# Causal attention stage: the sums' products moved in front of a run of the next half's value products

## The chip, the cores and the metric

The kernel runs on one core of a Trainium2 chip. The time is microseconds on the device from the start to the end of one execution; a lower one is better. Beside it stands one profiled execution, whose rows are read here.

## The reference, cut to what matters

`x` is 4 sequences of 1024 tokens with 512 channels. A layer with causal self-attention (16 heads of 32 channels), cross-attention to 64 context rows and a feed-forward block is followed by a second layer with a gate. Only the first attention is touched by the change:

```python
xn1 = _ln(x, g1, be1)
q, k, v = xn1 @ Wq + bq, xn1 @ Wk + bk, xn1 @ Wv + bv        # per head
scores = jnp.where(causal_mask, q @ k.T / scale, -jnp.inf)
attn = jax.nn.softmax(scores, axis=-1)
x = x + (attn @ v) @ W1 + b1
```

Everything is float32.

## The kernel before

**Tiling.** The causal stage handles 16 groups `g` (4 sequences by 4 groups of four heads). A group has two halves `c2` of 512 query tokens. For a half, key blocks `j` of 128 keys (4 of them in half 0, 8 in half 1) and heads `i` (4) give a scores product `sc` (line 805, transposed: keys on the partitions), then `ex` on ScalarE (line 918) writes the exponentials. Blocks on the diagonal are masked first by VectorE (`low`, line 1034), and their products are narrower: 512, 384, 256 and 128 columns.

**Values.** `pv` (line 817) is a run of four products, one per head: 128 keys by 32 channels, each written to its own 32 partitions of PSUM bank 7. TensorE so works in groups of 32 columns there, while all its other products of this stage use 96 to 128. The profile has two records for each such product, so a `pv` is x8.

**Sums.** The exponentials of block 0 are written into `esum[c2][i]` (`es` in the profile), those of the other blocks into a ring of 8 tiles `er`. GpSimd adds each ring tile onto `es` (line 677). When a half is complete, `fin` (line 826, index `f = 2 * g + c2`) multiplies a matrix of ones with the four `es` tiles, again four products of 128 by 32 into four groups of 32 partitions, 512 columns each. Then comes a chain: ScalarE copies the result into `esum[c2][0]` (line 929), `f0` (SyncE's queue) moves four rows of it into a small tile (line 609), `f1` is the reciprocal on VectorE (line 1043), `f1d` and `f2` spread it through DRAM into the tile `rs` (lines 613 and 619), `f3` on GpSimd multiplies the attention output by it (line 683), `f3d` stores 256 KB (line 624). The exponentials of block 0 of the same half of the next group overwrite `es`, so the first of them waits for the landing of `f0` (semaphore `d_cmp`, lines 916 and 917).

**Other work of the stage.** Row maxima of the coming group: products `mx` (line 762), reduced by VectorE (lines 1023 and 1027), turned by `mxT` (line 775). Projections `pj` and values `vm` in three passes (lines 55 to 57), normalised tokens transposed (`lnT`, line 739), and `stack`, DMAs of 256 KB, three per call, that rearrange queries and keys (line 599).

**Order.** All five engines walk one list, `order1()`, sorted by a planned time whose unit is one group; each takes its own steps from it, in order. `attn_steps` gives the steps of a half with weights and `spread` lays them evenly between the half's start and end (half 0 of group `g` is planned from `g` to `g + CUT`, half 1 from there to `g + 1`). `fin` and its chain are placed by fixed distances after the end of their half. `banks1` walks the same list and gives each PSUM use of the stage one of seven banks, the one free longest; a use waits for the release of the one before it in its bank (`free1`).

Of the kernel before, what the change touches and what calls it, by code (L numbers as in the profile page):

```python
# [72 lines left out]
def spread(start, end, steps):  # L73

    steps = list(steps)
    total, done, out = sum(c for _, c in steps), 0.0, []
    for s, c in steps:
        out.append((start + (end - start) * done / total, s))
        done += c
    return out  # L80


def ln_times(b, qt, ld, lnT):

    d = lnT - ld
    out = [(ld, ("ld", b, qt))] + [(ld + (0.36 + 0.06 * i) * d, ("st", b, qt, i)) for i in range(2)]
    out += [(ld + 0.5 * d, ("va", b, qt)), (ld + 0.56 * d, ("rs", b, qt))]
    out += [(ld + (0.68 + 0.08 * i) * d, ("nm", b, qt, i)) for i in range(2)]
    for kp in range(2):
        at = lnT + 0.05 * kp  # L90
        out += [(at, ("lnT", b, qt, kp)), (at + 0.01, ("lnh", b, qt, kp)), (at + 0.03, ("lnl", b, qt, kp))]
    return out


def proj_times(g, c2, wq, start, end):
    out = [(start + (end - start) * k / 4, ("pj", g, c2, wq, k)) for k in range(KT)]
    return out + [(end, ("pjh", g, c2, wq)), (end + 0.02, ("pjl", g, c2, wq))]


def max_steps(g, c2):  # L100
    for r, (ti, h0, per, c0, w, diag) in enumerate(MAXU):
        if ti // 4 == c2:
            yield ("mx", g, r), per * w + 100
    if c2:
        yield ("mxm", g), 300


def attn_steps(g, c2):

    nj = 4 * c2 + 4  # L110
    for j in range(nj + 1):
        for i in range(4):
            if j < nj:
                yield ("sc", g, c2, j, i), 512 - max(0, 128 * (j - 4 * c2)) + 60
            else:
                yield ("none",), 240
            if i == (3 if j > 4 * c2 else 2) and j:
                yield ("pv", g, c2, j - 1), 800 * (512 - max(0, 128 * (j - 1 - 4 * c2))) / 512
    yield ("none",), 200

# [3 lines left out]
CUT = (0.292, 0.27, 0.283, 0.294)  # L124
# [12 lines left out]
def order1():  # L137

    at0 = lambda us: (us - 72) / 58
    t = [(at0(a), s) for a, s in ((1.5, ("zld", 0)), (1.6, ("wld", 0)), (1.7, ("wld", 1)), (1.8, ("zld", 1)), (24.5, ("wld", 2)),  # L140
                                  (18, ("wh", 0)), (22, ("wh", 1)), (32, ("wh", 2)), (31, ("zp",)), (70, ("oh1",)), (15, ("msk",)), (20, ("ohc",)))]
    for qt in range(4):
        at, T0 = 4 + 2.5 * qt, 8 + 2.6 * qt
        t += [(at0(a), s) for a, s in ((1 + 0.1 * qt, ("ld", 0, qt)), (at, ("st", 0, qt, 0)), (at + 0.1, ("st", 0, qt, 1)),
                                       (at + 1, ("va", 0, qt)), (at + 1.2, ("rs", 0, qt)), (at + 2.6, ("nm", 0, qt, 0)),
                                       (at + 2.7, ("nm", 0, qt, 1)))]
        for kp in range(2):
            t += [(at0(T0 + 1.3 * kp), ("lnT", 0, qt, kp)), (at0(T0 + 1.3 * kp + 0.6), ("lnh", 0, qt, kp)),
                  (at0(T0 + 1.3 * kp + 1.2), ("lnl", 0, qt, kp))]
    for j in range(3):  # L150
        t += [(at0((18.5, 25, 45)[j] + (1.6, 1.6, 3.1)[j] * m), ("wb", j, m)) for m in range(4)]
    for u in range(13):
        at = 15.5 + 3.5 * u if u < 4 else 32 + 3 * (u - 4) if u < 8 else 45 + 3 * (u - 8)
        t += [(at0(at), ("z", u)), (at0(at + 2.5), ("ze", u))]
        if u < 4 or u in (8, 12):
            t.append((at0(at + 4), ("zo", u)))
    for b in range(1, NB):
        for qt in range(4):
            t += ln_times(b, qt, 4 * b + LN_LOAD[qt], 4 * b + LN_TURN[qt])
    for g in range(16):  # L160
        r = g % 4
        cut = CUT[r]
        at = [at0(a) for a in PROJ_0] if g == 0 else [g + a for a in (PROJ_1 if g == 1 else PROJ[r])]
        for c2 in range(2):
            for wq in range(2):
                n = 2 * c2 + wq
                t += proj_times(g, c2, wq, at[n], at[n] + (0.05 if g < 2 else PROJ_LONG[r]))
                back = g - 2 + (CUT[(g - 2) % 4] if n == 0 else CUT[(g - 2) % 4] + (1 - CUT[(g - 2) % 4]) * 0.54 if n == 1 else 1) + 0.03
                t.append((at[n] + 0.1 if g == 0 else max(at[n] + PROJ_LONG[r] + 0.07, back), ("stack", g, c2, wq)))
        if g % 2 == 0:  # L170
            for sp in range(4):
                s, d = (at0(VALUES_0[sp]), 0.05) if g == 0 else (g + VALUES[r // 2][sp], VALUES_LONG)
                t += spread(s, s + d, [(("vm", g // 2, sp, i), 1) for i in range(4)])
                t.append((s + d, ("ve", g // 2, sp)))
        m0, m1, end = (at0(46), at0(54), MAX_0) if g == 0 else [g + a for a in (MAX_1 if g == 1 else MAX[r])]
        t += spread(m0, m1, max_steps(g, 0)) + spread(m1, end, max_steps(g, 1))
        for c2, a in enumerate((m1, end)):
            t += [(a + 0.04, ("mxT", g, c2)), (a + 0.06, ("tq", g, c2)), (a + 0.09, ("tqd", g, c2))]
        for c2 in range(2):
            end = g + (1 if c2 else cut)  # L180
            steps = spread(g + cut * c2, end, attn_steps(g, c2))
            t += steps
            for a, s in steps:
                if s[0] == "sc" and s[3] >= 4 * c2 :
                    t += [(a + 0.014, ("low", *s[1:])), (a + 0.028, ("ex", *s[1:]))]
                elif s[0] == "sc":
                    t.append((a + 0.001, ("ex", *s[1:])))
            t += [(end + 0.02, ("sao", g, c2)), (end + 0.08, ("fin", 2 * g + c2))]
            t += [(end + a, (s, 2 * g + c2)) for a, s in ((0.14, "f0"), (0.26, "f1"), (0.3, "f1d"), (0.42, "f2"), (0.62, "f3"), (0.69, "f3d"))]
    t += order2()  # L190
    t.sort(key=lambda p: p[0])
    return t
# [152 lines left out]
def program(nc, A, out):  # L345
    top = ExitStack()
    with top:
# [84 lines left out]
        bt = cols[:, col_at["bt"]:col_at["bt"] + 4]  # L432
        BO = 7
        O1 = order1()
        Q.bank, Q.before, Q.last = banks1(O1)
        O1 = [s for _, s in O1]
# [1743 lines left out]
```

## Time and profile before

| | us |
|---|---|
| median of 3 runs | 2281.62 (2280.57 to 2282.13) |
| profiled execution | 2281.93 |
| its span | 2280.1 |
| causal stage, first value product to the last adds and sums | 114.4 to 984.7 |

The page's first part gives busy time by engine; its second part cuts the span into 40 slices, one digit of busy tenths each; its fourth part follows the chain of work that ended last. In the timeline each row is a start, a length, an engine, a line, an operation, what it writes and reads, and how many records were merged; brackets hold idle time of the engine before it and what ended it. Matmul records overlap, so the distance between starts, and not the length, is what a product occupies.

### The profile page before, as it was taken

How to read it: one execution, taken by the hardware profiler on the slowest of the kernel's cores; microseconds unless marked ns; L12 is line 12 of the kernel's file. 1: busy time of each engine (PE TensorE's matmuls, PEld its weight loads, DVE VectorE, ACT ScalarE, POOL GpSimd, SP SyncE). 2: the span in 40 equal slices, each digit the busy share in tenths (PEclk: the TensorE clock that was granted, in tenths of full speed). 3: DMA queues.
4: the chain of work that ended last, by engine and by line, in shares of the span. 5: the costliest groups of instructions: out<-in, count | busy, mean ns of one | idle time of the engine just before them, and what ended most of it. 6: DMA issues, size and time to landing. Idle time of an engine off the chain costs nothing.

```text
span 2280.1 us, 32164 instructions
## 1 busy us (share of the span) xinstructions
PE 2158.8 (95%) x11590; PEld 1604.1 (70%) x11590; DVE 1407.5 (62%) x3349; ACT 861.8 (38%) x1598; POOL 933.1 (41%) x943
## 2 busy tenths in 40 slices
PE   7999999999999997889999998999999999999996
PEld 5666666666656664467777776888887887888784
DVE  5577776876786678456666677443455546454546
ACT  4155655655565554533443333221211121121113
POOL 1067777777777777653333332001021201111212
PEclk9999999999999998899999999999999999999998
DMA  7655545555564564211111221320111121111101
GB/s 233 78 82 95 95 78 89 104 90 81 94 113 76 84 94 123 71 52 59 58 56 60 79 94 42 120 79 28 61 60 65 70 74 61 65 61 65 42 28 51
DMA packets 106323, 177.34 MB, mean 78 GB/s; under 512 B 18334, under 2 KB 23454, under 8 KB 106160
## 3 DMA queue, kind: packets, MB, share of 16 engines
q1 hardware_dynamic: 106164, 175.29, 33.1%
q8 instruction: 91, 1.49, 0.3%
q14 instruction: 68, 0.56, 0.1%
HBM read 83.67 MB, written 40.13 MB: 54 GB/s over the span
## 4 chain that ended last, share of the span: by engine, by line
PE 82%; DVE 7%; ACT 4%; issue 3%; POOL 2%; DMA 1%; SPq 0%; POOLq 0%; ACTq 0%; DVEq 0%
PE psum L55 19%; PE psum L56 18%; PE psum L57 18%; PE psum L817 6%; PE psum L762 6%; PE psum L805 5%; PE psum L720 1%; DVE psum L1023 1%; PE psum L826 1%; ACT sx L1369 1%; PE psum L1323 1%; PE psum L739 1%; PE psum L1315 1%; PE psum L1264 1%; ACT pT L1396 1%
## 5 line engine op out<-in xcount | busy, mean ns | idle before, releaser
L677 POOL TENSOR_TENSOR es<-es,er 128x512 f32<-128x512 f32 (+3 forms) x640 | 588.7, 955 | 266.5 <-PE psum L817 241.5
L918 ACT ACTIVATE er<-psum 128x512 f32<-128x512 f32 (+3 forms) x640 | 278.5, 471 | 299.8 <-DVE psum L1034 192.3
L1023 DVE CUSTOM_DVE_ANT_0 psum<-psum,mask_ts 128x384 f32<-128x384 f32 (+3 forms) x512 | 249.2, 502 | 151.7 <-PE psum L762 149.5
L805 PE MATMUL psum<-qs,ks 100*128 100x512 f32 (+3 forms) x768 | 251.0, 364 | 22.3 <-DVE mx L1023 18.7
L762 PE MATMUL psum<-ks,qs 96*128 96x512 f32 (+3 forms) x768 | 259.1, 369 | 5.8 <-DVE mx L1023 3.1
L1873 ACT ACTIVATE fy<-psum,cols 128x512 f32<-128x512 f32 x128 | 88.2, 689 | 452.4 <-PE psum L57 451.9
L762 PEld LDWEIGHTS psum<-ks,qs 96*128 96x128 f32 x768 | 139.6, 190 | 111.6 <-issue 32.9
L1027 DVE TENSOR_REDUCE mx<-psum 128x1 fp32r<-128x512 f32 x256 | 175.5, 685 | 59.5 <-PE psum L762 58.6
L55 PE MATMUL psum<-fh,hh 128*128 128x512 f32 x512 | 201.0, 393 | 7.1 <-DVE hl L1974 7.1
L55 PE MATMUL psum<-fah,fh 128*128 128x512 f32 x512 | 203.0, 397 | 0.0
L1972 DVE CAST hh<-fy 128x512 fp32r<-128x512 f32 x128 | 60.9, 476 | 229.8 <-ACT fy L1873 229.4
L57 PE MATMUL psum<-fah,fl 128*128 128x512 f32 x512 | 200.1, 391 | 0.0
L56 PE MATMUL psum<-fal,fh 128*128 128x512 f32 x512 | 199.9, 390 | 0.0
L57 PE MATMUL psum<-fh,hl 128*128 128x512 f32 x512 | 199.4, 390 | 0.0
L56 PE MATMUL psum<-fl,hh 128*128 128x512 f32 x512 | 199.3, 389 | 0.0
L805 PEld LDWEIGHTS psum<-qs,ks 100*128 100x128 f32 x768 | 143.0, 193 | 69.0 <-DVE mx L1023 31.3
L1238 POOL TENSOR_TENSOR pp<-pp,small 128x1024 f32<-128x1024 f32 x32 | 61.1, 1911 | 266.2 <-DVE small L1504 266.2
L1769 POOL TENSOR_TENSOR et<-et,vpb 128x512 f32<-128x512 f32 x24 | 35.4, 1477 | 284.9 <-ACT et L1899 284.9
L1034 DVE TENSOR_TENSOR psum<-psum,mask_st 128x128 f32<-128x128 f32 x512 | 138.2, 303 | 21.8 <-PE psum L805 21.1
L817 PE MATMUL psum<-er,v 128*32 128x512 f32 (+3 forms) x1280 | 137.8, 486 | 0.6 <-ACT er L918 0.4
L55 PEld LDWEIGHTS psum<-fh,hh 128*128 128x128 f32 x512 | 96.1, 188 | 28.9 <-DVE hl L1974 9.5
L57 PEld LDWEIGHTS psum<-fah,fl 128*128 128x128 f32 x512 | 96.4, 188 | 20.6
(258 smaller groups left out, 4593.0 us busy)
## 6 DMA issues: line engine op xcount, KB each, us to landing
qs<-stage SPq DMA_DIRECT2D x96, 256.0 KB, 5.7
ks<-stage SPq DMA_DIRECT2D x96, 256.0 KB, 8.2
rs<-rs_d SPq DMA_DIRECT2D x32, 256.0 KB
sa_d<-rs SPq DMA_DIRECT2D x32, 256.0 KB, 2.1
sx<-sa_d SPq DMA_DIRECT2D x8, 1024.0 KB, 5.7
xt<-in_x SPq DMA_DIRECT2D x32, 256.0 KB, 6.0
x_d<-xt SPq DMA_DIRECT2D x32, 256.0 KB, 2.0
fw<-in_Wf SPq DMA_DIRECT2D x16, 512.0 KB, 5.2
```

The source lines that it names most:

```text
L55: e.matmul(dst, lh, rh, start=start, stop=False)
L56: e.matmul(dst, lh, rl, start=False, stop=False)
L57: return e.matmul(dst, ll, rh, start=False, stop=stop)
L677: e.tensor_tensor(es, es, er, ALU.add).then_inc(s_add.sem, 1)
L762: t = e.matmul(bank1(*s)[:, v * wd:v * wd + wd], Q.qs[par][0:96, i, 128 * ti:128 * ti + 128], Q.ks[par][0:96, i, c0:c0 + wd], start=True, ...
L805: t = e.matmul(ps[:, off:512], Q.ks[par][0:100, i, 128 * j:128 * j + 128], Q.qs[par][0:100, i, 512 * c2 + off:512 * c2 + 512], start=True, ...
L817: e.matmul(bank[BO][32 * i:32 * i + 32, off:512], values(g)[:, j, h:h + 32], src[:, off:512], start=j == 0, stop=j == nj - 1).then_inc(s_p ...
L918: e.activation(dst, bank1("sc", g, c2, j, i)[:, off:512], ACT.Exp, scale=SCALE).then_inc(s_freeS.sem, 1)
L1023: t = e.tensor_tensor_reduce(out=ps, in0=ps, in1=mask_ts[:, 512 - wd:512], scale=1.0, scalar=-3e38, op0=ALU.add, op1=ALU.max, accum_out=mx ...
L1027: e.tensor_reduce(mx[:, at:at + 1], bank1(*s)[:, 0:wd], AX, ALU.max).then_inc(s_red.sem, 1)
L1034: e.tensor_tensor(ps, ps, mask_st[:], ALU.add).then_inc(s_low.sem, 1)
L1873: e.activation(y[:], ring3(("h", c, m)), ACT.Relu, bias=col("bf1", m), scale=1.0).then_inc(s_r3.sem, 1)
```

## The change

`fin` leaves its fixed place (0.08 group after the end of its half). It is now yielded by `attn_steps` of the next half, with weight 0, directly ahead of one of that half's `pv` runs: ahead of block 1 in half 0, and of block 2 in half 1. Its chain keeps its distances from `fin` (0.06, 0.18, 0.22, 0.34, 0.54 and 0.61 group). The last `fin` (31) and its chain stay where they were. The order of all other steps among themselves stays the same on every engine; since `banks1` walks the changed list, most uses get another bank (1332 of 1664).

```diff
+FIN_BESIDE = (1, 2)
+FIN_AFTER = (0.06, 0.18, 0.22, 0.34, 0.54, 0.61)
 def attn_steps(g, c2):
     nj = 4 * c2 + 4
...
             if i == (3 if j > 4 * c2 else 2) and j:
+                if j - 1 == FIN_BESIDE[c2] and (g or c2):
+                    yield ("fin", 2 * g + c2 - 1), 0
                 yield ("pv", g, c2, j - 1), 800 * (512 - max(0, 128 * (j - 1 - 4 * c2))) / 512
...
+    attn_order = {(g, c2): spread(g + CUT[g % 4] * c2, g + (1 if c2 else CUT[g % 4]), attn_steps(g, c2))
+                  for g in range(16) for c2 in range(2)}
...
-            steps = spread(g + cut * c2, end, attn_steps(g, c2))
+            steps = attn_order[g, c2]
...
-            t += [(end + 0.02, ("sao", g, c2)), (end + 0.08, ("fin", 2 * g + c2))]
-            t += [(end + a, (s, 2 * g + c2)) for a, s in ((0.14, "f0"), (0.26, "f1"), (0.3, "f1d"), (0.42, "f2"), (0.62, "f3"), (0.69, "f3d"))]
+            t.append((end + 0.02, ("sao", g, c2)))
+            if g == 15 and c2:
+                t.append((end + 0.08, ("fin", 31)))
+            fin = end + 0.08 if g == 15 and c2 else next(a for a, s in attn_order[g + c2, 1 - c2] if s[0] == "fin")
+            t += [(fin + a, (s, 2 * g + c2)) for a, s in zip(FIN_AFTER, ("f0", "f1", "f1d", "f2", "f3", "f3d"))]
```

## Rows read from the trace of the kernel before

**Rows 1.** The page: busy time, and two lines of its 40 slices.

```profile
PE 2158.8 (95%) x11590; PEld 1604.1 (70%) x11590; DVE 1407.5 (62%) x3349; ACT 861.8 (38%) x1598; POOL 933.1 (41%) x943
...
PE   7999999999999997889999998999999999999996
...
PEclk9999999999999998899999999999999999999998
```

**Rows 2.** The page: the chain that ended last, by engine.

```profile
PE 82%; DVE 7%; ACT 4%; issue 3%; POOL 2%; DMA 1%; SPq 0%; POOLq 0%; ACTq 0%; DVEq 0%
```

**Rows 3.** Busy time in stretches of the causal stage (records in brackets).

```profile
376.00:588.00 212.00, 207.74 (x1289) 136.76 (x1289) 155.30 (x516) 122.32 (x258) 160.95 (x179) 1.00 0.56 92
588.00:800.00 212.00, 207.48 (x1286) 136.44 (x1285) 155.33 (x513) 121.81 (x257) 160.57 (x179) 1.00 0.55 92
800.00:930.00 130.00, 113.56 (x638) 69.32 (x637) 94.24 (x268) 68.42 (x151) 96.56 (x100) 0.89 0.47 94
930.00:985.00 55.00, 48.03 (x198) 23.79 (x196) 24.71 (x51) 23.84 (x49) 37.52 (x35) 0.91 0.22 77
```

**Rows 4.** Timeline of TensorE around one sums run, of the half before.

```profile
590.52 0.40 PE L56 MATMUL psum<-xl,wqh 128*128 128x512 f32 x1
590.76 0.39 PE L57 MATMUL psum<-xh,wql 128*128 128x512 f32 x1
590.99 0.34 PE L805 MATMUL psum<-qs,ks 100*128 100x384 f32 x1
591.25 1.07 PE L826 MATMUL psum<-es,sm 128*32 128x512 f32 x8
592.25 0.44 PE L762 MATMUL psum<-ks,qs 96*128 96x384 f32 x1
592.53 0.52 PE L805 MATMUL psum<-qs,ks 100*128 100x384 f32 x2
```

**Rows 5.** Timeline of TensorE: an ordinary 384-column pitch, and value runs of 512 and 128 columns.

```profile
589.93 0.34 PE L762 MATMUL psum<-ks,qs 96*128 96x384 f32 x1
590.11 0.34 PE L805 MATMUL psum<-qs,ks 100*128 100x384 f32 x1
...
561.13 1.06 PE L817 MATMUL psum<-er,v 128*32 128x512 f32 x8
562.12 0.50 PE L762 MATMUL psum<-ks,qs 96*128 96x512 f32 x1
...
534.54 0.43 PE L817 MATMUL psum<-er,v 128*32 128x128 f32 x8
534.90 0.66 PE L762 MATMUL psum<-ks,qs 96*128 96x128 f32 x4
```

**Rows 6.** The line of the sums' products: ns min/median/max.

```profile
L826 PE MATMUL psum<-es,sm x256: 592/617/1062, 124.9 to 984.7; 128*32 128x512 f32 x128
```

**Rows 7.** Timeline of TensorE, 641.2 to 652 us: all rows with idle time.

```profile
643.34 0.44 PE L805 MATMUL psum<-qs,ks 100*128 100x384 f32 x1 [0.28 <-ACT es L918]
...
644.53 0.45 PE L805 MATMUL psum<-qs,ks 100*128 100x384 f32 x1 [0.76 <-DVE mx L1023]
...
648.16 0.63 PE L739 MATMUL psum<-ident,xr 128*128 128x128 f32 x4 [0.29 <-ACT xr L857]
...
650.98 0.50 PE L762 MATMUL psum<-ks,qs 96*128 96x512 f32 x1 [0.45 <-DVE mx L1023]
```

**Rows 8.** Timelines of SyncE's queue, TensorE and ScalarE around `f0` of half 11.

```profile
429.71 2.25 SPq L599 DMA_DIRECT2D ks<-stage  x3
...
432.77 0.57 SPq L609 DMA_DIRECT2D small<-es  x1
...
437.51 0.53 PE L817 MATMUL psum<-er,v 128*32 128x384 f32 x4
...
443.05 0.60 ACT L918 ACTIVATE es<-psum 128x512 f32<-128x512 f32 x1 [1.16 <-PE psum L805]
```

**Rows 9.** Half 27: issue of its `f0`, and the one exponential that waited for it.

```profile
854.37 0.58 SPq L609 DMA_DIRECT2D small<-es  x1
...
863.50 1.09 ACT L918 ACTIVATE es<-psum 128x512 f32<-128x512 f32 x2 [2.20 <-DMA small<-es]
```

**Rows 10.** The page: DMA issues by kind, the last number from issue to landing.

```profile
ks<-stage SPq DMA_DIRECT2D x96, 256.0 KB, 8.2
...
sa_d<-rs SPq DMA_DIRECT2D x32, 256.0 KB, 2.1
```

**Rows 11.** Timeline of GpSimd, 372 to 392 us.

```profile
372.19 1.26 POOL L683 TENSOR_TENSOR rs<-sao,rs 128x512 f32<-128x512 f32 x1
373.42 4.47 POOL L677 TENSOR_TENSOR es<-es,er 128x256 f32<-128x256 f32 x8
384.19 7.93 POOL L677 TENSOR_TENSOR es<-es,er 128x384 f32<-128x384 f32 x11 [6.30 <-PE psum L817]
```

**Rows 12.** Who waited for whom in the causal stage.

```profile
ACT es L929 <- PE psum L826: 9.7, 18, 1.2
...
ACT er L918 <- POOL es L677: 5.1, 10, 1.1
```

## The prediction

> **What bounds the kernel now.** I read the page first, for the engine that carries the span: TensorE is busy 95% of it, at full clock in nearly every slice [rows 1], and it makes 82% of the chain that ended last [rows 2]. An average says little about the stage that is changed, so the second view is busy time by stretch. Between 376 and 800 us TensorE is busy 207.74 of 212 us and 207.48 of 212 us, 98%, at a granted clock of 1.00 (the 2.4 GHz level), while VectorE has 73%, ScalarE 58% and GpSimd 76% [rows 3]. There a nanosecond that TensorE no longer needs is mostly a nanosecond of time. From 800 to 985 us it is busy 113.56 of 130 and 48.03 of 55 us, 87%, with the clock at 0.89 to 0.91 [rows 3]: other engines and transfers set the pace in part, and a saving is worth less.
>
> Third, the timeline of TensorE, for what one sums run costs. In it, only distances between starts count. The run of half 17 starts at 591.25 and the next product at 592.25 [rows 4].
>
> **The edit on TensorE.** The same 32 `fin` runs of 8 records are issued, so no product is removed. What goes is that a run of 32-column products stands alone between products of the full width. I price both situations.
>
> Alone: the product ahead of the run starts at 590.99 and is 384 columns wide; two such products otherwise stand 0.18 us apart (589.93 to 590.11, [rows 5]), but the run starts 0.26 us later: 0.08 on entering. The run holds the engine for 1.00 us (591.25 to 592.25). The product behind it, again 384 wide, is followed after 0.28 us (592.25 to 592.53) instead of 0.18: 0.10 on leaving [rows 4, 5]. Together 1.18 us.
>
> In a longer run: the trace has no sums run joined to a value run, so I bound it. Each record lasts 0.617 us and the eight together 1.07 [rows 4, 6], so the last starts about 0.45 us after the first: four products' first passes take 0.45, and eight records in a stream 0.90. That gives 1.18 - 0.90 = 0.28 us saved per join. Another way: a value run of 128 columns occupies 0.36 us (534.54 to 534.90), one of 512 columns 0.99 (561.13 to 562.12) [rows 5]; that is 0.63 us for 384 columns, 1.64 ns each, so 512 columns stream in 0.84 and 0.15 us is fixed. Then 1.18 - 0.84 = 0.34 us per join. From below: if what is fixed belongs to each group of four products whatever stands beside it, the 0.15 stays, and if entering and leaving are only late weight loads that a joined run has as well, nothing is saved: 0. Nothing in the rows makes a join dearer than standing apart, since both runs then have the same shape. I take 0.29, nearest to the value that comes from the starts inside a run.
>
> The Trainium skill has another account of the end of such a run ("TensorE: Matmul & The Clock Gate", section "The cost: per-tile semaphore tail"): increments serialise, about 25 + 4.7 per tile + 26.3 ns per increment. By that page a value run with its four increments would have a tail of 149 ns and a sums run with its single one 70 ns, an estimate from the page's formula. The trace doesn't bear that difference out: both occupy the same 0.99 to 1.00 us [rows 4, 5].
>
> Joins: all but the last of 32, so 31. Those of halves 0 to 27 land in the saturated part: 28 x 0.29 = 8.1 us. Halves 28 to 30 are in the last stretches at 87%: between 0 and 3 x 0.34 = 1.0; I take 0.3. Sum: -8.4 us.
>
> **What gives some back.** First, filler. Each `fin` moves later by 6 to 18 us: half 17's from 591.25 to its join, and half 11's to 437.51, where `pv` of block 1 starts [rows 8]. Between the two places TensorE arrives 1.18 us earlier at products whose banks VectorE or ScalarE must free. Where it already idles there, the idleness grows. In one group out of four it does: 0.28, 0.76, 0.29 and 0.45 us of idle time between 643 and 651 us, mostly for VectorE [rows 7]. The whole 1.18 us could turn into idle time there, of which the join then pays back nothing; in the other groups the idle rows are few, since all idle time of 424 us is 8.8 us [rows 3]. The loss is between 0 and 4 x 1.18 = 4.7 us; VectorE is busy only 73%, so it catches up in part, and I take 1.0.
>
> Second, the chain behind `fin`. Everything in it moves with it: the ScalarE copy, `f0`, `f1`, `f1d`, `f2`, `f3` and `f3d`. On VectorE the reciprocal keeps its 0.12 group behind `f0`; on ScalarE the copy waits for its products as it did 18 times for 9.7 us in all [rows 12], on an engine with 42% to spare. On GpSimd, `f3` of every first half leaves the densest part of the second half (372.19, with adds right behind it) and falls into the 6.30 us that GpSimd idles before the next group's first add [rows 11]: 1.26 us of relief per group for an engine that ScalarE waited for by 5.1 us in all [rows 12]. I count no gain for that. `f3` of a second half moves one block later in the same kind of row, price nothing.
>
> Third, the wait on `f0`. For a second half, its landing must come before the first exponential of the next group's second half. With half 11: `fin` now starts at 437.51 minus its own length, thus on the old clock about 437.5, the four products and the copy take 1.7 us (1.07 + 0.6), `f0` is issued near 439.3, and the exponential stands at 443.05 [rows 8]: 3.8 us are left. Unloaded, 2.1 us are enough even for 256 KB; but the small transfer goes behind `stack` transfers that take 8.2 us to land [rows 10]. In half 27 it took from 854.37 to about 863.5, 9.1 us, and the exponential waited 2.20 [rows 9]. Key transfers issued at 429.71 [rows 8] plus 8 to 10 us land near 439 to 441, so an `f0` issued at 439.3 lands hardly later than one issued at 432.77 did, except for one new thing: `f3d` of the first half, 256 KB, now goes into SyncE's queue between `stack` and this `f0`. Three stack transfers of 256 KB are issued in 2.25 us and take 8.2, so one such transfer in the backlog is worth 0.7 to 2.7 us. Added waiting per group is then between 0 and about 2 us of ScalarE, 0 to 30 us over 15 groups at the far end; what reaches TensorE is smaller, since the value products of block 0 come several products later. By the slack of 3.8 us I expect it to show only where stack's backlog was deepest, as in half 27: 0.4 us in sum.
>
> Fourth, banks. The new assignment is as crowded as the old: the same seven banks, the same steps. A `fin`'s own bank is now wanted soon after it, by scores products of block 3 about 1.3 to 2 us behind the old start of `pv` block 1; the added 0.9 us of the joined run keeps that just clear of the 1.7 us until the copy is done. Between -1 and +1.5 us; I take 0.
>
> **Sum.** -8.4 + 1.0 + 0.4 = -7.0 us. The profiled execution (2281.93; span 2280.1, 1.8 around it) would become 2274.9, and it stands 0.3 above the median of the runs, 2281.62, which becomes 2274.6.
>
> **The rivals.** Changes of up to 0.2%, 4.6 us, can hardly be told from none.
>
> *A: half of it given back.* The join saves 0.28, but TensorE waits for VectorE in more groups than the one in four. 1.18 us of lost filler in half of the 28 places, of which a quarter sticks, is 4 us: -8.4 + 4 to 6, so 2277 to 2279. For it speaks that VectorE is the next in the chain [rows 2] and the four idle rows [rows 7]; against it, that idle time is 2% [rows 3].
>
> *B: the change doesn't do what it says.* Fixed time belongs to each group of four products, or new weights in a joined run come late; a join saves 0 to 0.07 us, 31 x 0.07 = 2.2, less the 1.4 given back: 2280 to 2282. Against it: inside a run the second passes follow at 0.45 us though they have their own weights [rows 4, 6]. The Trainium skill's semaphore tail is of this kind: only a sums run's own 70 ns would be recovered.
>
> *C: slower, by the wait on `f0`.* One mechanism: `es` is free later than the first exponential of block 0. With `f3d` ahead and 9 us as in half 27 [rows 9] it would land at 448 instead of 443. It decides once the added wait exceeds 8.4 / 15 = 0.56 us of TensorE per group; at 1 us it gives 2281.6 - 8.4 + 1 + 15 = 2289. For it: one wait is there already [rows 9]. Against it: transfers ahead were issued 8 us earlier and drain in the meantime.
>
> **How the numbers follow.** Forecast 0.70, with its own range 2271.5 (31 x 0.34 = 10.5 and nothing given back gives 2271.1) to 2277; A 0.14; B 0.07; C 0.09, of which 0.02 stays within the bound. The range: 2271.5 to 2279.5 takes in the forecast and A and leaves out B, C and the edge. Faster by over 0.2% (below 2277.06): the forecast and some of A, 0.75. Within: most of A, B and the rest of C, 0.18. Slower: 0.07.
>
> **What the changed profile would show.** Right: in TensorE's timeline 31 places where x8 of line 826 is followed by x8 of line 817 with no full-width product between, the two starting about 0.9 us apart, and one entering and one leaving for both; the stage ending 7 to 8 us earlier, and all later stages as long as before. A: more idle rows ended by line 1023 between a half's start and the join. B: the value run starts 1.0 us or more behind the sums run. C: `ACT es L918` waiting for `DMA small<-es` in many groups instead of one. The forecast is wrong if the join shows a third pass that comes later than 0.45 us, or if ScalarE's copies now hold a bank that scores products of block 3 need.

## The result, and the profile after

Before: 2278.78 us, the median of 20 runs (2270.25 to 2285.31). After: 2283.54 us, the median of 20 (2278.21 to 2288.64). The ratio is 1.0025, 95% interval 1.0016 to 1.0033: the change costs 5.7 us of 2279, where 7.0 us of gain were forecast. (Here and below a ratio is taken over all runs, and the us beside it are that ratio on the median before. The difference of two medians can be another by up to 2 us; here it is 4.8. The twenty runs before have a median 2.8 us under that of the three runs the forecast started from, which doesn't change its sign.) The profiled execution after took 2283.22 us with a span of 2281.4 and a mean granted clock of 0.979; before it was 2281.93, 2280.1 and 0.984.

All line numbers after are 11 higher. The page after: busy time and chain by engine, to be read against [rows 1, 2], and two kinds of transfer against [rows 10].

```profile
PE 2162.4 (95%) x11590; PEld 1613.8 (71%) x11590; DVE 1402.9 (61%) x3349; ACT 861.8 (38%) x1598; POOL 934.2 (41%) x943
...
PE 83%; DVE 7%; ACT 4%; issue 3%; POOL 2%; DMA 1%; POOLq 0%; SPq 0%; DVEq 0%; ACTq 0%
...
ks<-stage SPq DMA_DIRECT2D x96, 256.0 KB, 7.1
...
sa_d<-rs SPq DMA_DIRECT2D x32, 256.0 KB, 6.5
```

The same 11590 products keep TensorE busy 3.6 us longer: work didn't go, it got slower. (The stores of the normalised halves land in 6.5 us instead of 2.1, since they now go among `stack`'s transfers. No compute engine waits for them; SyncE's own queue does, 12 times for 19.2 us in all, before 6 times for 12.0.)

The join itself does what it was said to. TensorE's timeline of half 17 after, which answers to [rows 4]:

```profile
592.72 0.28 PE L816 MATMUL psum<-qs,ks 100*128 100x256 f32 x1
592.93 1.06 PE L837 MATMUL psum<-es,sm 128*32 128x512 f32 x8
593.82 0.83 PE L828 MATMUL psum<-er,v 128*32 128x384 f32 x8
594.58 0.33 PE L816 MATMUL psum<-qs,ks 100*128 100x128 f32 x1
```

The value run starts 0.89 us behind the sums run, with 0.90 forecast, and no product of another shape stands between; the trace has 31 such joins. So look for where the gain went. Busy time in the stretches of [rows 3], with the granted clock as the third number from the end:

```profile
376.00:588.00 212.00, 207.81 (x1286) 138.60 (x1285) 154.62 (x510) 122.36 (x259) 160.06 (x176) 0.99 0.56 92
588.00:800.00 212.00, 207.81 (x1285) 138.68 (x1284) 154.60 (x512) 122.27 (x258) 160.09 (x176) 0.99 0.56 92
800.00:930.00 130.00, 116.77 (x626) 71.72 (x627) 90.06 (x256) 66.82 (x149) 97.07 (x99) 0.84 0.43 92
930.00:985.00 55.00, 47.57 (x193) 23.33 (x191) 23.37 (x50) 23.09 (x47) 37.26 (x34) 0.91 0.21 73
```

In each of the two full stretches the clock is 0.99 instead of 1.00 and TensorE gets through a few products fewer; from 800 to 930 us it is 0.84 instead of 0.89, and TensorE is busy 3.2 us longer with 12 records fewer.

Both kernels issue the same other products in the same order, so they can be lined up. The table is worked out from the traces: when a product starts, against the same product of the profiled execution before (us; the columns are the time there). Each kernel was profiled twice more for it.

```
                    427    849    870    984   2200   total of the run
before, again 1     0.0    0.0   +1.5    0.0   -0.3   2281.66
before, again 2    -0.9   +1.6   +1.6   -7.6   -5.4   2277.93
after              -3.0   -2.9   +0.3   +0.4   -0.2   2283.22
after, again 1     -1.6   -2.3   +1.8   -2.3   -2.3   2279.64
after, again 2     -2.0   -2.7   +1.1   +2.3   +2.5   2284.78
first halves only  -4.6   -6.7   -7.4  -16.9  -15.0   2268.35
```

Three things are to be seen. The kernel after is ahead by 2 to 3 us by 427 us and hardly more at 849, though 16 joins lie between. Between 849 and 870, the first half of group 14 and the start of its second, it loses 3.2 to 4.1 us (the kernel before 0.0, 1.5 and 0.0). And one execution of the kernel before gets 9 us in one place behind 870 that the others don't, so a single profile can't tell 5 us here; the verdicts below come from many runs.

Cut at the first scores product of each half, the same line-up says what a join does where. Differences in the length of halves against the profiled execution before, in us, summed over the groups named; the last four rows are kernels of the experiments below:

```
                    first halves of groups       second halves  1st half of  2nd half of
                    odd 3 to 13   4,8,12   6,10  3 to 13        group 2      group 14
before, again 1         0.0        0.0    +0.1     0.0            +0.1          +0.5
before, again 2         0.0        0.0    +2.6    +0.1            -1.4          -8.8
after                  -0.7       +0.9    +3.0    -3.4            -0.9          +0.3
after, again 1         -0.7       +1.0    +2.2    -3.4            -0.5          -1.7
after, again 2         -0.7       +1.0    +2.2    -3.6            -0.7          +1.5
first halves only       0.0        0.0    +0.8    -3.3            -3.5         -10.8
old banks              -0.2       +1.1    +5.3     0.0            -0.3          +2.3
before, late split      0.0        0.0    +0.4    +0.6            -3.5         -10.9
filler back            -0.7       +0.9    +1.4    -3.5            -0.6          +1.9
```

Eleven joins in second halves give 3.4 to 3.6 us, 0.31 each (unevenly: 1.0 in groups 6 and 10, 0 to 0.3 in the others). Eleven joins in first halves cost 2.4 to 3.2 us: those of odd groups give 0.12 each, those of groups 4, 8 and 12 cost 0.3 each, and those of groups 6 and 10 cost 2.2 to 3.0 together. What the last two columns show comes and goes without the change: the first half of group 2 is 3.5 us shorter in the kernel "before, late split", whose order is that of the kernel before up to group 14.

Where the rest of the 0.29 goes is to be seen in group 9 (and in 5, but not in 3, 7 and 11). TensorE after, then before:

```profile
595.84 0.60 PE L816 MATMUL psum<-qs,ks 100*128 100x128 f32 x2
596.37 0.64 PE L828 MATMUL psum<-er,v 128*32 128x256 f32 x8
```

```profile
598.96 0.34 PE L805 MATMUL psum<-qs,ks 100*128 100x128 f32 x2
599.23 0.64 PE L817 MATMUL psum<-er,v 128*32 128x256 f32 x8
```

Two scores products of block 3 now take 0.53 us to the next run instead of 0.27: the second waits for an exponential, on a ScalarE that has had the sums' copy (0.60 us from 594.07) in between. That the copy is the reason wasn't tested.

Between 427 and 849 the losses sit in the first halves of groups 6 and 10: 1.6 us between 427 and 442 us in all three executions of the kernel after. TensorE's timeline there, all rows with idle time ([rows 7] has the same place in group 10 before):

```profile
426.50 0.50 PE L816 MATMUL psum<-qs,ks 100*128 100x512 f32 x1 [0.45 <-DVE mx L1034]
...
429.24 0.44 PE L816 MATMUL psum<-qs,ks 100*128 100x384 f32 x1 [0.97 <-ACT es L929]
...
430.18 0.44 PE L773 MATMUL psum<-ks,qs 96*128 96x384 f32 x1 [0.50 <-DVE mx L1034]
```

The second of them, in this group before:

```profile
432.26 0.44 PE L805 MATMUL psum<-qs,ks 100*128 100x384 f32 x1 [0.28 <-ACT es L918]
```

One wait of 0.28 us has become 0.97. In sum the idle rows of this half are the same, 1.92 us in three where the kernel before has five (0.45, 0.28, 0.50, 0.29 and 0.45, 1.97 us): what was lost isn't idle time. Then windows of 20 us around three such first halves, first of the kernel before, then of the one after:

```profile
426.00:446.00 20.00, 17.96 (x115) 11.12 (x115) 18.66 (x72) 14.12 (x35) 12.78 (x21) 1.00 0.76 135
636.00:656.00 20.00, 17.70 (x123) 10.62 (x122) 18.55 (x74) 13.92 (x35) 13.84 (x23) 1.00 0.73 135
856.00:876.00 20.00, 18.83 (x108) 9.42 (x108) 14.67 (x50) 12.78 (x29) 16.48 (x19) 1.00 0.77 175
```

```profile
426.00:446.00 20.00, 17.85 (x98) 10.92 (x98) 17.19 (x68) 12.95 (x28) 10.85 (x16) 0.91 0.77 126
636.00:656.00 20.00, 17.85 (x100) 11.11 (x99) 17.06 (x68) 13.25 (x29) 10.70 (x16) 0.91 0.76 145
856.00:876.00 20.00, 17.37 (x85) 9.50 (x89) 12.51 (x39) 10.62 (x25) 13.34 (x16) 0.83 0.67 194
```

TensorE's busy time is nearly the same in the first two, but behind the longer wait the clock stands at its lower level (1.2 GHz) for part of the window and fewer products are done. In group 6 it does so in all three executions (0.93, 0.83 and 0.86 from 433 to 443 us, 1.00 before). What that adds can be read from the other executions: in the two where the stretch 644 to 654 us has a clock of 1.00, the first half of group 10 loses 0.6 us between 640 and 654; in the profiled one, where it has 0.90, it loses 1.3. The kernel before has the same price: in its second repeat the clock is 0.80 from 639 to 656 us instead of 1.00, and that half takes 2.6 us longer with the same order.

The longer wait and the lower clock go together, though not always. From 427 to 444 us the clock is under 1.00 in 10 of the 11 profiles whose sums are joined in group 6's first half, and in 3 of the 9 whose sums stand alone there; from 639 to 656 us in 8 of 11 and 1 of 9.

In group 14 the wait of [rows 9] has grown from 2.20 to 3.97 us (2.83 and 2.58 in the repeats before, 4.85 and 4.55 after). ScalarE, then TensorE, whose next product waits for it:

```profile
862.93 1.08 ACT L929 ACTIVATE es<-psum 128x512 f32<-128x512 f32 x2 [3.97 <-DMA small<-es]
```

```profile
861.10 0.22 PE L773 MATMUL psum<-ks,qs 96*128 96x128 f32 x1
863.58 0.49 PE L816 MATMUL psum<-qs,ks 100*128 100x512 f32 x1 [2.26 <-ACT es L929]
```

This gave two theories for the runs. **Filler:** in the first halves of groups 2, 6, 10 and 14 TensorE waits for VectorE and ScalarE, so the lone sums run there cost nothing; joined, it costs up to its 0.89 us, and where the wait grows the clock falls. **The wait on `f0`**, rival C, in group 14 alone. Beside them: the banks, and the place of the join.

### The profile page after: what moved, and what is told of

It reads as the page before. It is cut to its first block, busy times and chain, and to the rows that moved or that the text cites. A ratio compares the mean times of both kernels' runs of the same rounds, so it can differ in the third digit from the quotient of the medians.

```text
span 2281.4 us, 32165 instructions
## 1 busy us (share of the span) xinstructions
PE 2162.4 (95%) x11590; PEld 1613.8 (71%) x11590; DVE 1402.9 (61%) x3349; ACT 861.8 (38%) x1598; POOL 934.2 (41%) x943
## 4 chain that ended last, share of the span: by engine, by line
PE 83%; DVE 7%; ACT 4%; issue 3%; POOL 2%; DMA 1%; POOLq 0%; SPq 0%; DVEq 0%; ACTq 0%
PE psum L55 19%; PE psum L56 18%; PE psum L57 18%; PE psum L828 7%; PE psum L773 7%; PE psum L816 5%; PE psum L731 1%; PE psum L837 1%; DVE psum L1034 1%; ACT sx L1380 1%; PE psum L1334 1%; PE psum L750 1%; PE psum L1275 1%; PE psum L1326 1%; ACT pT L1407 1%
```

## The experiments

Each is the kernel after with the edit shown, unless said otherwise; ratios are to the kernel before on the same chip. Four ask for one part of the change at a time, or for another place and other banks. `joined(f)` says which halves' sums are joined; the others stay at the old place, with the old chain behind them.

```
+def joined(f):
+    return f % 2 == 0        # e1; e2: f % 2 == 1, with f2, f3, f3d of first halves +0.13
-FIN_BESIDE = (1, 2)
+FIN_BESIDE = (0, 2)          # e3
-    b = min((k for k in range(7) if ends[use] < until.get(k, 99)), key=lambda k: free[k])
+    b = fixed[use] if fixed and use[0] != "fin" else min(...)   # e4: banks of the order before
```

**First halves' sums alone joined** (16 joins):

> Only the sums of first halves are joined to a value run (16 joins, all in second halves); those of second halves stand alone at their old place, 0.08 group into the next first half. Theory A (lost filler: the sums taken out of the first halves leave TensorE idle there, in every fourth group the granted clock falls to 1.2 GHz behind it, and in group 14 the exponentials wait longer for f0): 16 x 0.29 = 4.6 us saved and nothing of A's cost, 2 to 5 us faster than before, granted clock 1.00 in the stretches 640 to 650 us. Theory B (the new banks cost time all over the stage): no faster than before, within 1.5 us. Theory C (the first half's 256 KB store now goes ahead of the second half's f0): the wait of group 14 grows from 2.2 to about 4 us although f0 is issued early, and the gain is 1 to 3 us.

Measured: 2272.68 against 2279.43, ratio 0.9962 (0.9947 to 0.9976), -8.7 us; more than any of its theories gave. The medians are 6.8 us apart, and its times run from 2264.3 to 2277.4.

**Second halves' sums alone joined** (15 joins, which land in the next group's first half; `f2`, `f3` and `f3d` of first halves had to move too, so this kernel differs in two things):

> Only the sums of second halves are joined (15 joins, in the next group's first half); those of first halves stand alone at their old place, with f2, f3 and f3d of theirs 0.13 group later, since the queue would otherwise wait in a circle. Theory A: it carries the whole cost and half of the saving: 3 to 10 us slower than before, clock at 1.2 GHz near 430, 642 and after 860 us, ScalarE waiting about 4 us for f0 in group 14. Theory B (banks): like e1, within 1.5 us of before. Theory C: about 2 us slower.

Measured: 2291.61, 1.0049 (1.0035 to 1.0063), +11 us.

**Second halves' sums joined one value run earlier:**

> All 31 joins, but in first halves ahead of the value run of block 0 instead of block 1: the sums lose 3 us less of their early place and f0 is issued about 3 us earlier. Theory A: the filler moves back by half the distance and the wait of group 14 falls from 4.0 to about 2 us; 3 to 8 us faster than before. Theory B: as slow as the change, +2 to +6 us. Theory C: the wait of group 14 stays near 4 us, since the store is still ahead, and the time is 0 to 4 us above before.

Measured: 2284.07, 1.0017 (1.0005 to 1.0029), +3.9 us, where the filler theory had 3 to 8 us of gain. The wait on `f0` in its profile is 2.79 us.

**Banks as before for all but the sums:**

> The change with the banks of the kernel before for every use except the sums' own, which take the bank that is free longest. Theory A: as the change, +3 to +8 us. Theory B: the loss is gone, 5 to 8 us faster than before. Theory C: as the change.

Measured: 2292.38, 1.0051 (1.0038 to 1.0064), +11.6 us.

The first pair is the finding of the study: the change is a gain and a loss, and the loss is all in the second halves' sums. The two parts don't quite add (-8.7 and +11 against +5.7, each with 2 to 3 us of uncertainty). The size of the gain isn't that of the joins: 4.5 us stand in the second halves of groups 0 to 13 of its profile, and most of the rest of its lead in the first half of group 2 and in group 14, where the kernel before has it in some executions. The place of the join hardly matters. The new banks aren't the loss: without them it doubles. In that kernel's profile the second halves of groups 3 to 13 gain 0.0 us where they gained 3.4, over half of the 5.9 us by which it is slower than the change. So a join there pays only together with its new banks; the banks without the joins weren't run.

The next four separate group 14's wait from the filler: undo the join of half 27 alone, or of halves 3, 11, 19 and 27, whose sums fall into the first halves of groups 4k + 2; or keep all joins and shorten the wait on `f0` by taking transfers from in front of it in SyncE's queue.

```
+    return f != 27           # e5; e6: f % 8 != 3
-FIN_AFTER = (0.06, 0.18, 0.22, 0.34, 0.54, 0.61)   # e7: 0.71 for f3d of first halves
-CROSS_ONCE = (14.168,        # e8, and the third first load 0.042 later: both behind f0 of half 27
+CROSS_ONCE = (14.262,
```

> The change, but the sums of half 27 stand alone at their old place in group 14. Theory D (the loss is made in group 14, where the exponentials wait 4.0 us for f0 behind two loads of the next stage and a store, and the granted clock falls at 864 us): that wait is back at 2.2 us, no half clock before 880 us, and the time is 1 to 4 us below before. Theory A (the lost filler costs in every fourth group, the clock at 1.2 GHz near 431 and 643 us): those stretches stay as in the change, and half or more of the 5.7 us loss stays: +2 to +5 us.

Measured: 2278.37 against 2280.02, 0.9993 (0.9977 to 1.0010), -1.6 us. Its twelve times lie in two clumps, six from 2271.2 to 2275.5 and six from 2281.3 to 2287.2, so the median says little. The wait on `f0` is down to 2.70 us, and the clock still falls behind it (0.66 from 866 to 876 us), which theory D had ruled out.

> The change, but the sums of halves 3, 11, 19 and 27 (the first halves of groups 2, 6, 10 and 14) stand alone at their old place: 27 joins are left. Theories A and D both: no fall of the clock near 431 and 643 us that the kernel before does not have, f0 waits as before, and 4 to 8 us faster than before. Should the joins themselves have a hidden price, the time stays within 1.5 us of before or above it.

Measured: 2273.92, 0.9979 (0.9962 to 0.9995), -4.8 us: 10.5 better than the change with four of 31 joins undone. These times too lie in two clumps, seven from 2267.0 to 2275.9 and five from 2279.2 to 2281.2, with the profile in the lower. And its clock falls at 430 us (0.85 from 423 to 433), with the sums of half 11 at their old place.

> The change, but every first half's 256 KB store f3d stands 0.10 group later, behind the second half's f0 in the queue. Theory C (the store ahead makes f0 late): the wait of group 14 falls from 4.0 us to 2.5 or less, and 2 to 4 us of the loss are gone. Theory D with the loads of the next stage as the cause: the wait stays at 3.5 us or more. Theory A: the clock near 431 and 643 us is unchanged by it.

Measured: 2290.17, 1.0045 (1.0029 to 1.0062), +10 us; the wait is still 3.99 us. The store isn't what delays `f0`. Why it is slower than the change stays open.

> The change, but two loads of the next stage (512 KB of context, 256 KB of a weight) stand behind f0 of half 27 in the queue instead of ahead of it; the stores stay ahead. Theory D with the loads as the cause: the wait of group 14 falls from 4.0 to about 2 us, no half clock at 864 us, 2 to 4 us of the loss are gone. Theory C: the wait stays at 3.5 us or more.

Measured: 2285.07, 1.0028 (1.0016 to 1.0040), +6.4 us. The wait is down from 3.97 to 2.5 us, near the 2.20 of before, and the time isn't better. So the wait on `f0` exists and is longer, but it isn't what costs the 5.7 us.

The repeated profiles were run next (in the table above). They showed one more suspect. In group 14 a VectorE instruction stands still for some 10 us behind a long row of GpSimd adds, and TensorE behind it. The profile after, by VectorE's, GpSimd's and TensorE's timelines:

```profile
876.25 9.59 DVE L1426 TENSOR_TENSOR W1l<-raw,W1h 128x512 fp32r<-128x512 f32 x1
...
886.85 0.67 DVE L1426 TENSOR_TENSOR W1l<-raw,W1h 128x512 fp32r<-128x512 f32 x1
```

```profile
869.26 14.81 POOL L688 TENSOR_TENSOR es<-es,er 128x512 f32<-128x512 f32 x12 [6.66 <-PE psum L828]
```

```profile
886.43 0.79 PE L816 MATMUL psum<-qs,ks 100*128 100x512 f32 x1 [7.80 <-DVE mx L1034]
```

The next such instruction takes 0.67 us. This standstill is in two of three executions of the kernel before, in three of three after, and not in the profiles of e1 and e6; those of e2 to e5, e7 and e8 have it. Theory E: the change makes it certain, and that is the loss. To test it, the split of the cross stage's weights is moved out of group 14 in four kernels alike: before, after, first halves only, four apart.

```
-CROSS_LOAD = (14.019, 14.431, 14.754, 14.309, 15.318)
+CROSS_LOAD = (14.019, 14.431, 15.16, 14.309, 15.318)
-            t += [(at + 0.04 * k, ("2wh", j, k)), (at + 0.04 * k + 0.05, ("2wl", j, k))]
+            t += [(at + 0.04 * k, ("2wh", j, k)), (at + 0.04 * k + 0.05 if j == 2 else (15.02, 15.18)[j] + 0.03 * k, ("2wl", j, k))]
```

> The kernel before, with VectorE's part of the first two weight splits of the next stage moved from group 14 into group 15 (and a load that reuses their buffer after it). Theory E (VectorE stands still for 8 to 10 us in group 14 while GpSimd adds, and TensorE waits for it): no operation of VectorE over 3 us, and 4 to 9 us faster than before. If that standstill is hidden anyway: within 2 us of before.

> The change with the same move. Theory E (the change loses because it meets the standstill in every execution and the kernel before only in some): it comes out 1 to 3 us faster than the kernel before with the same move. Theories A and D (lost filler and the clock, whatever VectorE does): it stays 3 to 6 us slower than the kernel before with the same move.

> Only first halves' sums joined, with the same move. Theory E: the lead of this placement (8.7 us, measured where its profile has no standstill) shrinks to 3 to 5 us against the kernel before with the same move. Theories A and D: the lead stays 6 us or more.

> 27 joins (halves 3, 11, 19 and 27 apart), with the same move. Theory E: 2 to 5 us faster than the kernel before with the same move, near the kernel with first halves alone. Theories A and D: the same lead, since neither keeps the fins of the critical groups.

Measured, against 2278.62 before:

```
before + late split               2273.01   0.9977 (0.9966 to 0.9988)
after + late split                2278.11   0.9997 (0.9985 to 1.0008)
first halves only + late split    2267.27   0.9951 (0.9936 to 0.9965)
four apart + late split           2270.96   0.9967 (0.9954 to 0.9981)
```

With the late split the change still costs 5.1 us (2278.11 - 2273.01), as without it, and undoing the four joins gives back 7.2 (2278.11 - 2270.96, no clumps now). So theory E falls as the cause of the loss. It has a part in the gains: the late split alone is worth 5.2 us, the lead of first halves alone shrinks from 8.7 to 5.7, between what E and what A and D gave, and that of the four apart from 4.8 to 2.1, as E gave and not A and D. One reservation: in all four profiles another VectorE instruction now has a standstill. Here it is without the change (eight copies of the kernel before with the late split, the longest 9.1 us):

```profile
888.66 10.51 DVE L1426 COPY pp<-ctc 128x256 f32<-128x256 f32 x8
```

The last two test the filler theory directly. **Filler back:** the kernel after, with one 384-column scores product issued six extra times in the first half of groups 2, 6, 10 and 14, into a bank that the real one then overwrites. By its pitch of 0.18 us [rows 5] that is an estimated 24 x 0.18 = 4.3 us of added work.

```
+                    for _ in range(6 if g % 4 == 2 and s[2:] == (0, 1, 0) else 0):
+                        e.matmul(ps[:, off:512], ..., start=True, stop=True)
```

> The change, with the scores product of head 0, block 1 issued six times more ahead of itself in the first halves of groups 2, 6, 10 and 14, about 1.1 us of TensorE where the sums stood; the sums stay joined and late. It is work that the kernel before did not have, 4.3 us in all. Filler theory: the idle time there is filled and the granted clock holds as in the kernel before, so this comes out at or below the change, -3 to +1 us against it (+2 to +6 against before). Lateness theory: the added work costs its full length, +3 to +5 us against the change (+9 to +11 against before).

Measured: 2284.88 against 2279.02, 1.0022 (1.0009 to 1.0034), +5.0 us; the change alone is at +5.7. At their full length the added products would have made it +10 us, and the interval ends at +7.7: they cost nothing that can be measured. Windows of this kernel:

```profile
426.00:446.00 20.00, 18.21 (x115) 11.79 (x112) 17.82 (x68) 13.40 (x30) 11.67 (x19) 1.00 0.83 147
636.00:656.00 20.00, 18.22 (x118) 11.66 (x117) 17.80 (x69) 13.41 (x32) 12.10 (x19) 1.00 0.79 147
856.00:876.00 20.00, 16.22 (x85) 8.75 (x77) 11.28 (x37) 9.49 (x22) 12.44 (x16) 0.83 0.74 195
```

In groups 6 and 10 the clock is back at 1.00, the wait of 0.97 us at 0.26, and 115 and 118 records of products are done, the added ones included (115 and 123 before, 98 and 100 after). The two first halves cost 1.4 us instead of 2.2 to 3.0. In group 14 the clock still falls to 0.83, and `f0` is waited for by 4.95 us. One execution can't say more, and the time of the whole is that of the change.

**More joins on top of the best kernel:** first halves and the second halves of groups 4k and 4k + 2, whose sums fall into first halves outside the four, with the late split.

```
+    return f % 2 == 0 or f % 8 in (1, 5)
```

> All first halves' sums joined and those second halves' whose join falls into groups with g % 4 of 1 or 3 (24 joins), with the weight splits moved. If a join outside the critical groups gains its 0.2 us: 1 to 2 us below the kernel with first halves alone and the same move, thus 12 to 13 us under before. If a late sum costs what its join saves: the same as that kernel, 11 us under before.

Measured: 2269.76, 0.9962 (0.9948 to 0.9977), -8.7 us, against -11.2 with the 16 joins of first halves alone (measured at different times on different chips; the intervals overlap). More joins in first halves add nothing that can be measured. In the profile those of odd groups give their 0.12 us each, and 2.9 us are lost in the first halves of groups 6 and 10, where nothing was joined, at a clock of 0.80 from 427 to 444 us.

The version to keep is first halves only with the late split: 2267.27 us, 11 us faster than the kernel before and 16 faster than the one after.

## Why the prediction was wrong

**What held.** The engine that bounds the stage, the 31 joined runs, the 0.89 us between the starts, and the price of a join where the sums of first halves go: 0.31 us on average in second halves against 0.29. The average is in part luck, since groups 6 and 10 give 1.0 each, half of it an idle row of 0.52 us that is gone, and others nothing, and since the old banks bring it to 0. Rival B is false as a rule for all joins; those of odd first halves come near it.

**The step that failed** is "What gives some back. First, filler", with its 1.0 us: it rests on "VectorE is busy only 73%, so it catches up in part". With it goes the half of "28 x 0.29" that lies in first halves: in groups 3 to 13, where 3.2 us of gain were counted for them, they cost 2.4 to 3.2. Three things were wrong.

First, the sign of a join there. I charged at most the loss of the 1.18 us that was saved. But in the first halves of groups 2, 6, 10 and 14 TensorE isn't the bound, which e13 shows: 4.3 us of added products are free there. A lone sums run would have been as free. Moved to the joined run, behind those waits, it costs: the rows have 0.6 us lost in group 10 at full clock, and in group 14 up to 862 us, where 0.3 gained had been counted.

Second, idle time was priced at its length. With a wait of 0.97 us instead of 0.28 the granted clock is 0.91 over 20 us, and where group 10 has the lower clock its loss is 1.3 instead of 0.6 us. That the wait brings the clock down was not shown by itself: e1 and e6 have a fall near 430 us without it, and with products in its place (e13) the clock is up in the one execution profiled. In group 14, from 849 to 870, the loss is 3.2 to 4.1 us; the profiles of e1, e6 and of the four apart with the late split have none there. Undoing the four joins improves the time by 10.5 us (7.2 with the late split, the firmer number).

Third, [rows 3] average over four groups. A busy share of 98% holds for three groups and hides a first half of the fourth in which TensorE waits four times for others [rows 7]. The 28 "saturated" joins were 14 in second halves, which gained, and 14 in first halves, which together with the last one cost 11 us when made alone.

Rival A named the right place ("TensorE waits for VectorE") and was mis-sized: 4 to 6 us given back, where the forecast's own saving and the result are 14 us apart (-8.4 to +5.7). Rival C forecast the sign: its wait came in one group, not fifteen, at 3.97 instead of 2.20 us, and shortening it to 2.5 gave nothing back. ScalarE's wait for GpSimd's adds before it can write `er` again, 5.1 us in [rows 12], tells nothing:

```profile
ACT er L929 <- POOL es L688: 13.3, 11, 2.3
```

That is the profile after; the repeats have 12.7 and 4.6 us after, and 7.1 and 10.2 before. The fourth step, banks at 0, wasn't the loss; keeping the old ones would have cost 6 us more. Its sign of being wrong appeared in part: in groups 5 and 9 a scores product of block 3 waits, for an exponential and not for the copy itself.

**What stays open.** How group 14's loss divides between waiting and clock: e13 mends the clock in groups 6 and 10 but not there, and its time is that of the change. Why the joins of groups 4, 8 and 12 cost 0.3 us and those of second halves gain between 0 and 1.0. What decides whether VectorE stands still in an execution, and how much of the medians' difference is the kernel before escaping it now and then: the three profiles of each kernel end only 2.1 us apart in the mean of their spans (2278.7 and 2280.8), less than the 5.7 of the medians. And whether the two parts of the change really fail to add, or only scatter.

## What to carry to other kernels

A saving on the bounding engine is worth its length only in the stretches where that engine is the one waited for. Before work is moved, look at the idle rows of both its old and its new place, one period of the pattern at a time: work that stands in a wait is free, and it isn't free where it goes. And when a change has parts that land in different stretches, time the parts alone: here one half of it was worth 6 to 9 us and hid inside a loss.

## What the runs showed of the hardware

Two VectorE operations stood for 7.5 to 10.4 us while GpSimd added without a pause: the TENSOR_TENSOR of the rows above, which otherwise takes 0.67 us (9.8 us before, 9.6 after, behind adds of 1.27 us each), and a copy whose seven neighbours take 0.28 us (9.1 us in e9, behind adds of 0.44 to 1.25). In e1, where it doesn't happen, the same TENSOR_TENSOR takes 1.1 to 1.7 us and the GpSimd adds around it 1.27 to 1.74, so the two take turns:

```profile
870.65 1.43 DVE L1433 TENSOR_TENSOR W1l<-raw,W1h 128x512 fp32r<-128x512 f32 x1
...
876.19 1.70 DVE L1433 TENSOR_TENSOR W1l<-raw,W1h 128x512 fp32r<-128x512 f32 x1
```

It comes and goes between executions of one kernel (9.8 and 10.2 us in two of the kernel before, not in the third). The Trainium skill ("SBUF — State Buffer", section "Who interferes with whom") has the two engines share a pair of ports under an exclusive lock; an operation with two SBUF inputs would then wait for the GpSimd instruction that holds it. The turns in e1 agree with that; a standstill across seven or eight adds in a row is more than that page says.

The time itself scatters by 15 us from run to run in the kernel before (2270.25 to 2285.31), and the granted clock of 22 runs of it lay between 0.981 and 0.986. With 5 to 20 runs of a kernel the 95% intervals still reach 2 to 4 us either way. The clock's level is part of the scatter: with one and the same order the first half of group 2 takes 3.5 us less at a granted clock of 1.00 (before, late split) than at 0.82 from 213 to 232 us (before).
